# Order of the two kinds of part in a square product's matmuls: woven in quarters, or one kind and then the other

## The reference

```
xn = layernorm(x)
s  = random-feature attention of xn with input_weights, xis, proj_matrix     # exp of dots, then a 256x256 product
h  = silu(xn W1 * s1) * (xn W2 * s2)                                         # 256 -> 1024
h  = gelu(h H1 * s3)                                                         # 1024 -> 1024, "layer 0"
h  = gelu(h H2 * s4)                                                         # 1024 -> 1024, "layer 1"
g  = silu(h W3 * s5)                                                         # 1024 -> 256
out = x + s * g
```

## Time and profile before

| what | value |
|---|---|
| median of three runs | 1252.62 us |
| the profiled execution | 1251.94 us, of which 1250.1 us are the span of its instructions |
| mean granted clock of TensorE | 0.998 |
| busy: TensorE, VectorE, ScalarE, GpSimd | 99%, 83%, 75%, 23% |
| matmuls, of them in `product` (L1010) | 5976, 3584 (1792 high, 1792 low) |
| one product, start to start | 7.14 us, 14 of them in a tile |
| `product` in all: 112 products | about 800 us of the span |

### The profile page before, as it was taken

One profiled execution on the slowest core, in us unless ns is written; L12 is line 12 of the kernel. 1 busy time (PEld: TensorE's weight loads), 2 busy tenths in 40 slices (PEclk: granted clock), 3 DMA queues, 4 the chain that ended last, 5 costly groups with the idle time before them and its releaser, 6 DMA issues.

```text
span 1250.1 us, 16620 instructions
## 1 busy us (share of the span) xinstructions
PE 1241.9 (99%) x5976; PEld 820.6 (66%) x5976; DVE 1034.5 (83%) x1427; ACT 934.4 (75%) x1426; POOL 281.4 (23%) x325
## 2 busy tenths in 40 slices
PE   9999999999999999999999999999999999999997
PEld 7666676666766666666666666666676666766666
DVE  8889889887898888978888888888888888887775
ACT  5466767778677796778878778787787877787664
POOL 7985122030220302203022030220303112040000
PEclk9999999999999999999999999999999999999999
DMA  9689942575234851358414483145831557315441
GB/s 342 247 315 300 346 162 84 170 216 191 91 102 157 245 179 68 109 178 243 153 68 143 144 267 129 68 144 167 253 119 68 172 157 245 108 52 168 148 147 36
DMA packets 97352, 209.49 MB, mean 168 GB/s; under 512 B 13424, under 2 KB 16624, under 8 KB 96240
## 3 DMA queue, kind: packets, MB, share of 16 engines
q1 hardware_dynamic: 80032, 156.98, 38.2%
q0 software_dynamic: 17232, 51.39, 13.1%
HBM read 175.78 MB, written 38.83 MB: 172 GB/s over the span
## 4 chain that ended last, share of the span: by engine, by line
PE 99%; DVE 1%; ACT 0%; issue 0%; POOL 0%; POOLq 0%
PE ps L1010 64%; PE ps L938 12%; PE ps L1072 9%; PE ps L965 4%; PE ps L847 4%; PE ps L1045 0%; PE ps L1042 0%; PE ps L1034 0%; PE ps L1031 0%; PE ps L1026 0%; PE ps L1038 0%; PE ps L1023 0%; PE ps L1089 0%; PE ps L885 0%; DVE rows L1904 0%; PE ps L891 0%
## 5 line engine op out<-in xcount | busy, mean ns | idle before, releaser
L1010 PE MATMUL ps<-split_hi,ring 128*128 128x512 f32 x1792 | 453.6, 404 | 0.0
L1010 PE MATMUL ps<-split_lo,ring 128*128 128x512 f16 x1792 | 406.3, 380 | 0.0
L1010 PEld LDWEIGHTS ps<-split_hi,ring 128*128 128x128 f32 x1792 | 336.7, 188 | 82.6 <-DMA ring<-in_h 0.8
L1690 DVE SCALAR_TENSOR_TENSOR split_lo<-quad,split_hi 128x1024 f16<-128x1024 f32 x224 | 281.6, 1268 | 108.4 <-ACT split_hi L1238 108.3
L1010 PEld LDWEIGHTS ps<-split_lo,ring 128*128 128x128 bf16 x1792 | 166.5, 98 | 214.2 <-issue 27.5
L1238 ACT ACTIVATE split_hi<-quad 128x1024 fp32r<-128x1024 f32 x224 | 232.5, 1049 | 43.0 <-PE ps L1010 31.9
L1282 ACT ACTIVATE quad<-quad,cols_s 128x512 f32<-128x512 f32 x192 | 136.5, 719 | 50.0 <-DVE quad L1724 23.0
L1716 DVE TENSOR_TENSOR quad<-quad 128x1024 f32<-128x1024 f32 x128 | 161.4, 1289 | 0.7
L661 POOL TENSOR_TENSOR quad<-quad,s 128x256 f32<-128x256 f32 x56 | 45.5, 840 | 413.1 <-ACT quad L1274 413.1
L645 POOL DMA_DIRECT2D z_h<-xin x56 | 55.6, 1000 | 154.2 <-DVE xin L1547 154.2
L1290 ACT ACTIVATE quad<-ps 128x512 f32<-128x512 f32 x64 | 38.2, 597 | 36.1 <-PE ps L1010 36.1
(11 more groups left out here) (212 smaller groups left out, 1839.9 us busy)
## 6 DMA issues: line engine op xcount, KB each, us to landing
ring<-hs SPq DMA_DIRECT2D x428, 256.0 KB, 3.8
xin<-in_x SPq DMA_DIRECT2D x16, 512.0 KB, 4.2
s_h<-s SPq DMA_DIRECT2D x16, 512.0 KB, 4.2
seen<-in_h POOLq DMA_DIRECT2D x32, 256.0 KB, 4.4
res<-in_x SPq DMA_DIRECT2D x15, 512.0 KB, 4.9
out<-res SPq DMA_DIRECT2D x15, 512.0 KB, 2.6
z_h<-xin POOLq DMA_DIRECT2D x56, 128.0 KB, 6.2
xT_hi<-z_h POOLq DMA_DIRECT2D x14, 512.0 KB, 7.0
```

The source lines that it names most:

```text
L1010: mm = e.matmul(ps[:, 4 * (w % 2) + m, :], weights, moving, start=first and k == 0 and begins, stop=last and k == Q - 1 and not begins, sk ...
L1690: e.scalar_tensor_tensor(out=both(slots_lo[i], g), in0=both(quad[at[t][L][FAST[w][1]]], g), scalar=POWER[L], in1=both(slots_hi[i], g).bitc ...
```

## The change

In tiles 1 to 7 a product takes all four turns of one kind and then all four of the other. Products 0, 2, 4 and 6 of layer 0 and 1, 3 and 5 of layer 1 begin with the low kind, the others with the high kind, so that each begins with the kind that its predecessor ended with. Tile 0 is as before. `WOVEN`, a list of products that would keep the old order, is empty. Nothing else changes; ScalarE's, VectorE's, GpSimd's and SyncE's instructions are the same in the same order.

```
+LOW_FIRST = [(0, 0), (0, 2), (0, 4), (0, 6), (1, 1), (1, 3), (1, 5)]
+WOVEN = []
...
                 on.wait_ge(hi, n_split(t, L, w, 1))
-
-                for m, g in [(m, g) for two, parts in ((0, (0, 1)), (2, (1, 0))) for g in parts for m in (two, two + 1)]:
-                    begins = g == m // 2
+                if t == 0 or (L, w) in WOVEN:
+                    turns = [(m, g) for two, parts in ((0, (0, 1)), (2, (1, 0))) for g in parts for m in (two, two + 1)]
+                else:
+                    begin = int((L, w) in LOW_FIRST)
+                    turns = [(m, g) for g in (begin, 1 - begin) for m in range(Q)]
+                for i, (m, g) in enumerate(turns):
+                    begins = all(v != m for v, _ in turns[:i])
                     if begins:
                         bank_free(t, L, w, m)
                     if g:
```

## The result

The changed kernel takes 1302.16 us, the median of five runs (1301.84 to 1306.90), against 1252.62 before (also the median of five, 1251.31 to 1253.44): 1.0405 of the time before, 95% interval 1.0393 to 1.0417. It is 49.5 us slower; 42.4 slower were forecast (1295), and the range of 1282 to 1312 holds it.

A forecast was written before the change was run, and what follows sets the result against it. TensorE, busy 99% of the span, was taken as the bound. Waits of 6.5 us in six tiles and 5.5 in the last made +44.7, less a gain of 2: +42.7 on 1252.62, forecast 1295, range 1282 to 1312.

The forecast's parts named there:

- A: Layer 0, product 5 waits for bank m = 2 (0.84 us) and bank m = 3 (1.90), 2.7 us a tile.
- E: Layer 1, product 5 waits for bank 3, 1.7 us a tile.
- The other products have cover: Products beyond A to E don't wait: their low halves are ready before they are wanted, their banks read earlier.
- C: Layer 1, product 3 waits for `low`, with a gelu between copy and `high` in product 2, 1.1 us a tile.
- D: Layer 1, product 5 waits for `low`, as B with no gelu between, 0.5 us a tile.
- The bound of 13 us from the idle weight loads: Upper bound of the gain: 49 fewer changes of kind at 0.26 us each, if that idle time were all TensorE's.
- B: Layer 1, product 1 waits for the second `low`, delayed by the later copy in product 0, 0.5 us a tile.
- the restart: Time to restart TensorE after a wait, taken as 0.1 us, one short weight load; bounds 0 and 0.2.
- Rival 1: Queues absorb the delay; only what is late at today's times waits, 2.3 us a tile: 1267 us; 8%.
- Rival 2: No wait at all and longer runs pay, a gain of up to 3 us: 1249.6 us; 2%.
- Rival 4: Delays pile up; product 6 of layer 1 or 0 waits too, 1 to 3 us a tile more: 1302 to 1316; 8%.
- Rival 3: TensorE's clock falls after waits, twice a tile (A and E), 3.0 us each, 42 us in all: 1337 us; 6%.

The follow-up runs named there:

- e2: The changed kernel with layer 0 back in the old woven order and only layer 1 in the new one; 1280.02 us (1.0222 of the kernel before).
- e5: The changed kernel; in tiles 1 to 7 both halves of the next product's `high` and `low` stand at m = 0, ahead of the `prod` step; 1279.21 us.
- e6: e5 with layer 0's last subtraction moved to product 3 and six small layernorm operations to product 5; 1273.19 us.
- e7: e6 with the second half of b11's split (`high_last`, `low_last`) moved from product 4 to 5 of layer 1; 1262.35 us.
- e9: e7 with layernorm entries moved and layer 1's first split issued whole at m = 0 of layer 0, product 6; 1250.3 us (0.9975 of the kernel before).
- e10: The changed kernel with only product 5 of both layers in the old woven order; 1279.67 us (1.0208 of the kernel before).
- e3: The kernel before with two changes from high to low in each product instead of one, 112 more; 1256.17 us (1.0030).
- e1: The changed kernel with layer 1 back in the old woven order and only layer 0 in the new one; 1277.9 us (1.0198 of the kernel before).
- e8: e7's moved queue entries with the old woven order of turns in all tiles; 1252.78 us (1.0001 of the kernel before).

## Why the prediction was right

**The bound and the sign.** TensorE had no idle time, so the gain could only be what a change of kind costs, and every wait moved forward had to be met by queues that nobody had moved. That held: five waits appeared, A to E, at the places named, and one of about 1 us beyond them, once in the kernel: `down` behind the gelu of tile 7's last product. It is in every run whose product 6 of layer 1 has the new order (e2, e5, e6, e7, e9, e10) and in none of the others. "The other products have cover" left out what comes behind the products. e10 shows for A and E that it is the place where a bank is wanted, e5 for C and D that it is the place of the split behind `prod`.

**The pace and the gain.** Forecast: 0.01 us a change and a faster late part of each run, 0.5 to 3 us, taken as 2. Measured on e9: 3.4 us in TensorE's stream, somewhat over the bounds by the starts, and 3.05 by the medians. In a run of 32 highs, 16 late ones at 0.2266 us instead of 0.2297 are 0.05 of the 0.07 us that two products gain, which is the faster late part that the prediction read in the earlier trace rows. The bound of 13 us from the idle weight loads is out by e3.

**The terms.** A was 2.7 forecast, 2.9 measured; C 1.1 and 1.3; D 0.5 and 0.65; E 1.7 and 1.5. All within 0.2. **B was mis-sized, 0.5 against 1.15.** In the prediction it is the step "second `low` 6.32 to 7.54", which lets VectorE wait for `high`. With layer 0 in its old order, in e2, that is what happens (product 0 starts at 573.56):

```profile
578.67 2.41 DVE L1698 SCALAR_TENSOR_TENSOR split_lo<-quad,split_hi 128x1024 f16<-128x1024 f32 x2
578.77 1.05 ACT L1246 ACTIVATE split_hi<-quad 128x1024 fp32r<-128x1024 f32 x1
```

The two low halves take 2.41 us instead of 2.35, as the second starts at 6.29, just behind `high`, and ends at 7.52. In the changed kernel product 0 starts at 586.33:

```profile
591.98 2.35 DVE L1698 SCALAR_TENSOR_TENSOR split_lo<-quad,split_hi 128x1024 f16<-128x1024 f32 x2
```

They run from 5.65 to 8.00 without a gap, 0.57 later than before (5.08 to 7.43): VectorE's own queue is the chain. It is late because the prediction carried layer 1's queue forward from today's time. Product 6 of layer 0 has a new order too, and on ScalarE the second half of `high` for product 0 stands behind the gelu of its m = 0. Before (product 6 starts at 558.27) and now (579.20):

```profile
563.50 1.04 ACT L1238 ACTIVATE split_hi<-quad 128x1024 fp32r<-128x1024 f32 x1
564.58 1.23 DVE L1690 SCALAR_TENSOR_TENSOR split_lo<-quad,split_hi 128x1024 f16<-128x1024 f32 x1 [0.91 <-ACT split_hi L1238]
583.78 0.69 ACT L1304 ACTIVATE quad<-ps,cols_s 128x512 f32<-128x512 f32 x1 [0.55 <-PE ps L1018]
584.98 1.05 ACT L1246 ACTIVATE split_hi<-quad 128x1024 fp32r<-128x1024 f32 x1
586.07 1.22 DVE L1698 SCALAR_TENSOR_TENSOR split_lo<-quad,split_hi 128x1024 f16<-128x1024 f32 x1 [1.57 <-ACT split_hi L1246]
```

The gelu now waits for TensorE, `high` starts 5.78 into product 6 instead of 5.23, and the low half behind it 0.57 later. From the start of this low half to that of the next two VectorE has 5.91 us of work without a gap, subtractions and layernorm above all, before and after, so the 0.57 stays. In tile 7, without the layernorm, it is made good, and product 0 is 7.76 (7.77 in e2). So of the 0.65 us that B is too small, 0.5 is this path, and 0.15 the restart.

**The restart.** Taken as 0.1 us. Behind a bank wait TensorE's next matmul starts 0.06 after the add, and the step after it is about 0.11 longer; at a product's start, with several semaphores to pass, the first matmul comes 0.25 after the low half (594.59 against 586.33 + 8.01). Three of those a tile at 0.15 more are 3 us in all.

**The sum.** 7.4 us of waits a tile instead of 6.5, of which B is 0.65 (its restart included) and the restarts of C and D most of the rest. Over seven tiles that is about 6 us. The wait of `down` adds at least 1 and the larger gain takes 1.4 back, which leaves some 6 of the 7 us between 1295 and 1302.2.

**The rivals.** Rival 1 (the queues absorb it) is out: A alone is 2.9, not 1.1. Rival 2 is out for the changed kernel; e9 is the kernel for which it holds, at 1250.3 against 1249.6 given. Rival 4 is out as priced: no further product waits, and the last bound is missed by `down` only once, at 1 us and not 1 to 3 a tile. But its kind of error, delays carried from one product to the next, is what made B too small. Rival 3, the clock, was given 6% and was right in kind. The prediction says that the granted clock stays at 1.00 throughout, and that it is wrong if the clock shows 0.5 inside the tiles. That sign came: the clock falls at A's second wait, in two of seven tiles of the profiled execution and five of seven in e1. It cost 3.0 us of the profiled execution, so the forecast time stands, but the sentence on the clock was wrong. The rival was wrong in place and price: never at E, whose single wait is 1.3 us, and 1.35 to 1.65 us a fall instead of 3.0. The reason that I gave against it, 2 us idle at full clock at the end of the kernel, doesn't hold for two waits that follow each other with four matmuls between. The rule cited from the Trainium skill with it ("TensorE: Matmul & The Clock Gate", on PSUM-queue depth-cycling) therefore agrees with these traces, where waits for banks stand between groups of matmuls, but only in part of the tiles; at D's and E's waits it doesn't show.

## What to carry to other kernels

An order of matmuls is a contract with the engines that make their inputs and drain their banks: when a stream without idle time is reordered, list for each semaphore how far its raising moves back and its wait moves forward, and carry each in-order queue between the two through by hand. Where rows of a queue stand back to back, the queue itself is the chain: an earlier input for its last entry helps nothing (e5), and what counts is when its first entry could start. So carry a queue on from where the product ahead leaves it in the new order, and follow it past the last product too. If the new order is worth a little on the bound engine, move the queue entries first (here those of e7 cost nothing, e8) and the turns after.

## What the runs showed of the hardware

- A float32 matmul of 512 columns with its own weight load starts about 0.231 us after the one before in the first ten of a run, and 0.2266 in the rest, in runs of 32 as in runs of 16; a low one 0.216, but for the first step of a run, 0.227. A change of kind by itself is nearly free: with 112 more of them e3 loses 3.8 us, some 0.03 each, the shorter runs' slower start included.
- The granted clock fell from 2.4 to 1.2 GHz behind two waits of 0.54 and 1.63 us idle with four matmuls between, in some tiles and not in others with the same waits: in five of six tiles in e1 and in two of six in the changed kernel. In tile 7, where these waits are 0.91 and 0.54 us, it stayed at 2.4, as it did throughout e10, whose largest single idle is 1.1 us. In two of the seven falls it came 0.5 us before TensorE's second wait ended, as in tile 3 of e1, shown below. What makes the difference from tile to tile stays open; no run was made for it.

```profile
564.00:564.25 0.25, 0.00 (x0) 0.00 (x0) 0.25 (x2) 0.20 (x1) 0.00 (x0) 1.00 0.00 0
564.30:564.70 0.40, 0.00 (x0) 0.00 (x0) 0.40 (x2) 0.00 (x0) 0.00 (x0) 0.50 0.00 0
```
